# Row maxima of the attention stage from the high parts alone: two chunks side by side in the two row halves of TensorE's array

## The reference, cut to what matters

```python
q = jnp.einsum('qdh,bcd->bhcq', Q, x) * sq
k = jnp.einsum('qdh,bcd->bhcq', K, x) * sq
v = jnp.einsum('vdh,bcd->bhcv', V, x) * sv
att = jnp.einsum('bhcq,bhCq->bhcC', q, k) / d_query
att = jnp.where(causal, att, -jnp.inf)
p = jax.nn.softmax(att, axis=-1)
y = jnp.einsum('bhcC,bhCv->bhcv', p, v)
z = jnp.einsum('dvh,bhcv->bcd', W, y) * (math.sqrt(d_embed / d_value) / num_heads)
```

## Time and profile before

| | |
|---|---|
| median of 3 runs | 2350.81 us (2349.38 to 2351.51) |
| profiled execution: own time, span | 2350.51 us, 2348.7 us |
| TensorE matmul busy, weight loads | 2008.2 us (86%), 1419.8 us (60%) |
| VectorE, ScalarE, GpSimd busy | 1377.0 us, 1007.6 us, 1166.8 us |
| attention stage | about 740 to 2050 us of the span |

### The profile page before, as it was taken

The page is one execution under the profiler, slowest core; times in us unless marked ns, Lnnn a source line. Parts: engine busy times, 40 slices in busy tenths (PEclk is TensorE's granted clock), DMA queues, the critical chain, the costliest instruction groups (busy, mean ns, idle before and its releaser), DMA issues. The chain is left out here.

```text
span 2348.7 us, 42315 instructions
## 1 busy us (share of the span) xinstructions
PE 2008.2 (86%) x11537; PEld 1419.8 (60%) x11538; DVE 1377.0 (59%) x3643; ACT 1007.6 (43%) x2116; POOL 1166.8 (50%) x1160
## 2 busy tenths in 40 slices
PE   4653999998957999989999989999999999956650
PEld 2352666665635777767777767777667777645550
DVE  7753333332345666665777665778656778647761
ACT  2210333332323555555555544555545555513540
POOL 0055222222211665643668753667744677826882
PEclk8855999999977999999999989999999999967985
DMA  8194222234240111111122101112102121123978
GB/s 306 65 291 173 43 47 45 45 82 109 45 136 18 47 47 50 46 30 44 47 69 52 47 27 45 49 51 53 47 22 53 44 56 45 38 90 122 198 115 239
DMA packets 234313, 186.45 MB, mean 79 GB/s; under 512 B 102826, under 2 KB 222471, under 8 KB 232592
## 3 DMA queue, kind: packets, MB, share of 16 engines
q1 hardware_dynamic: 200816, 149.15, 21.9%
q0 software_dynamic: 29088, 30.89, 8.2%
q10 hardware_dynamic: 4224, 4.19, 0.5%
HBM read 101.74 MB, written 82.95 MB: 79 GB/s over the span
## 5 line engine op out<-in xcount | busy, mean ns | idle before, releaser
L884 POOL TENSOR_TENSOR c_den<-c_den,c_p 128x512 f32<-128x512 f32 (+3 forms) x576 | 551.1, 957 | 358.8 <-ACT c_p L1113 288.0
L1113 ACT ACTIVATE c_p<-PS 128x512 f32<-128x512 f32 (+3 forms) x768 | 350.2, 487 | 349.4 <-PE PS L2183 237.1
L2204 PE MATMUL PS<-c_p,c_vh 128*64 128x256 f32 (+1 forms) x2816 | 336.1, 352 | 0.0
L2152 PE MATMUL PS<-c_k,c_q 128*128 128x512 f32 (+2 forms) x768 | 290.8, 380 | 29.9 <-DVE c_max L1606 20.4
L2175 PE MATMUL PS<-c_q,c_k 128*128 128x512 f32 (+2 forms) x768 | 292.9, 385 | 3.1 <-issue 1.9
L827 POOL DMA_INDIRECT acc<-b_y,b_tok x72 | 111.1, 1543 | 331.7 <-ACT b_y L1024 303.5
L2054 PE MATMUL PS<-b_w12T,b_tT 128*128 x576 | 272.9, 597 | 1.5 <-ACT b_tT L1007 0.7
L2204 PEld LDWEIGHTS PS<-c_p,c_vh 128*64 128x64 f32 x2816 | 198.4, 137 | 107.0 <-issue 53.5
L2176 PE MATMUL PS<-c_q,c_k 128*128 128x512 f32 (+2 forms) x768 | 259.0, 348 | 0.0
L1104 ACT ACTIVATE c_q<-PS 64x512 fp32r<-64x512 f32 x256 | 150.9, 590 | 176.2 <-PE PS L2139 173.0
L1613 DVE CUSTOM_DVE_ANT_0 PS<-PS,c_maskq 128x128 f32<-128x128 f32 (+3 forms) x256 | 127.0, 501 | 145.3 <-PE PS L2152 139.1
(11 more groups left out here) (286 smaller groups left out, 3611.2 us busy)
## 6 DMA issues: line engine op xcount, KB each, us to landing
c_vh<-c_v SPq DMA_DIRECT2D x64, 256.0 KB
c_rrow<-rden SPq DMA_DIRECT2D x64, 256.0 KB, 3.5
b_xt<-routed SPq DMA_DIRECT2D x72, 130.0 KB, 2.1
routed<-b_empty SPq DMA_DIRECT2D x32, 289.0 KB, 7.6
d_xe<-routed SPq DMA_DIRECT2D x32, 289.0 KB, 3.9
b_w12T<-in_w12T_dram SPq DMA_DIRECT2D x16, 512.0 KB, 12.7
acc<-X SPq DMA_DIRECT2D x16, 512.0 KB, 2.9
X<-acc SPq DMA_DIRECT2D x16, 512.0 KB, 9.5
```

The costliest lines, as they stand in the source:

```text
L884: pool.tensor_tensor(c_den[c][:, off:], c_den[c][:, off:], p, ALU.add).then_inc(s_cPa, 1)
L1113: act.activation(c_p[:, P_AT[m]:P_AT[m] + WIDTH[m]], PS[:, ST_BANK[m % ROUND], skip:skip + WIDTH[m]], ACT.Exp, scale=ATT_SCALE).then_inc(s ...
L2152: pe.matmul(PS[:, 2 + use[0], 0:max(w, 256)], c_q1[h][:, t * P:(t + 1) * P], c_k1[h][:, c * 512:c * 512 + max(w, 256)], start=True, stop=T ...
L2204: ins = pe.matmul(dst, c_vh[h][:, j, :], moving, start=(j == 0), stop=(t0 == 2 + a))
```

## The change

The chunks of the first pass multiply high parts alone: each matmul is 64 rows deep. Even chunks use rows 0 to 63 of `c_q1` and `c_k1`, odd chunks rows 64 to 127 of `c_q1` and `c_k2`, so that two neighbouring chunks stand in different row halves of the array. In the built program such a matmul has the tile size 64 x 128, at row 0 or row 64. For this `c_k2` has the high keys in rows 64 to 127, written by a fourth ScalarE copy from bank 0, and the ones in row 0; `c_q2` has the low queries in rows 64 to 127 and the maxima in row 0. GpSimd's copy goes. The chunks are issued in pairs, and the order on TensorE changes for it.

```diff
@@ SyncE
-                sp.dma_start(c_q2[h][DQ:DQ + 1, :].rearrange("a (t q) -> a t q", t=QT).bitcast(F32),
+                sp.dma_start(c_q2[h][0:1, :].rearrange("a (t q) -> a t q", t=QT).bitcast(F32),
@@ GpSimd
-            def copy_k(H, h):
-                pool.wait_ge(s_cqs, H * 6 + 6)
-                pool.sem_inc(s_pass, 1)
-                pool.tensor_copy(c_k2[h][0:DQ, :], c_k1[h][0:DQ, :].bitcast(F32)).then_inc(s_ck2, 1)
-                    if m == 4 and (nxt or hd + 1 < NH):
-                        copy_k(H + 1, 1 - h)
@@ ScalarE
-                            (c_k1[h][0:DQ, cols], PS[DQ:P, 0, :]))[part]
+                            (c_k1[h][0:DQ, cols], PS[DQ:P, 0, :]), (c_k2[h][DQ:P, cols], PS[DQ:P, 0, :]))[part]
-                    splits_hi(0, 2)
+                    splits_hi(0, 2, 3)
-                splits_hi(1, 0, 1, 2)
+                splits_hi(1, 0, 1, 2, 3)
@@ VectorE
-                dst, rows, hi = ((c_q2[h][0:DQ, cols], slice(0, DQ), c_q1[h]), (c_k1[h][DQ:P, cols], slice(DQ, P), c_k1[h]))[k]
-                dve.wait_ge(s_cqs, H * 6 + (c * 3 + k + 2))
-                dve.tensor_tensor(dst, PS[rows, 0, :], hi[0:DQ, cols].bitcast(F32), ALU.subtract).then_inc(s_cks, 1)
+                dst, rows, hi = ((c_q2[h][DQ:P, cols], slice(0, DQ), c_q1[h]), (c_k1[h][DQ:P, cols], slice(DQ, P), c_k2[h]))[k]
+                dve.wait_ge(s_cqs, H * 8 + (c * 4 + 2 * k + 2))
+                dve.tensor_tensor(dst, PS[rows, 0, :], hi[rows, cols].bitcast(F32), ALU.subtract).then_inc(s_cks, 1)
@@ TensorE
-                pe.matmul(PS[:, 2 + use[0], 0:max(w, 256)], c_q1[h][:, t * P:(t + 1) * P], c_k1[h][:, c * 512:c * 512 + max(w, 256)],
-                          start=True, stop=True).then_inc(s_cS, 1)
+                half = slice(n % 2 * DQ, (n % 2 + 1) * DQ)
+                pe.matmul(PS[:, 2 + use[0], 0:max(w, 256)], c_q1[h][half, t * P:(t + 1) * P],
+                          (c_k1, c_k2)[n % 2][h][half, c * 512:c * 512 + max(w, 256)], start=True, stop=True).then_inc(s_cS, 1)
-                    pe.wait_ge(s_ck2, H + 1)
...
-                maxima(4)
+                maxima(4, 5)
                 scores_t(H, h, 4)
-                maxima(5)
...
-                maxima_ahead(0)
+                denominators(H, 0)
+                maxima_ahead(0, 1)
                 projections(5)
-                maxima_ahead(1)
-                denominators(H, 0)
                 outputs_of(2)
```

More of the change, by code:

```diff
@@ L391, in network @@
         s_cks = sem("c_qk_lo_ready")
-        s_ck2 = sem("c_k2_ready")
         s_cv = sem("c_v_ready")
@@ L513, in batch_order @@
                 fetch = nxt and hd == NH - 2
-                order = ["M4", "M5", "M6"] * follows + ["X0", "X1"] * fetch + ["M7"] * follows
+                order = ["M4", "M5", "M6", "M7"] * follows + ["X0", "X1"] * fetch
                 order += ["Z2", "Z3"] * (zs and hd % 2 == 1)
@@ L904, in _ @@
                 pool.tensor_copy(dst, r_swb[:, cols]).then_inc(s_dcast, 1)
-            pool.wait_ge(s_cset, 3)
-            copy_k(0, 0)
             batch_adds(0, False, True)
@@ L1055, in _ @@
             for m in c_q2 + c_k2:
-                st.done(act.activation(m[DQ:P, :], zeros[DQ:P, 0:1].broadcast_to([P - DQ, S]), ACT.Copy))
+                st.done(act.activation(m[0:P - DQ, :], zeros[0:P - DQ, 0:1].broadcast_to([P - DQ, S]), ACT.Copy))
             st.sync()
@@ L1159, in head_exps @@
                     take_xT(b + 1, 1, table)
-                    splits_hi(0, 0, 1, 2)
+                    splits_hi(0, 0, 1, 2, 3)
                 take_y(H, pair, h, 0, c_yT[hp % 2])
@@ L1192, in _ @@
             for H, c in ((0, 0), (0, 1), (1, 0)):
-                for part in range(3):
+                for part in range(4):
                     split_hi(H, H, c, part)
             take_max(0, first_turns())
-            for part in range(3):
+            for part in range(4):
                 split_hi(1, 1, 1, part)
@@ L1767, in head_steps @@
                     invert(H - 1, 1 - h)
-                maxima(6)
+                maxima(6, 7)
                 if fetch:
                     low_xT(b + 1, 0, table)
-                maxima(7)
                 if h == 1 and zs:
@@ L1825, in _ @@
             for h in range(2):
-                st.done(dve.memset(c_k2[h][DQ:DQ + 1, :].bitcast(F32), 1.0))
+                st.done(dve.memset(c_k2[h][0:1, :].bitcast(F32), 1.0))
             st.sync()
@@ L2297, in head_products @@
                 scores_t(H, h, 5)
-                maxima(6)
                 if fetch:
+                    maxima(6, 7)
                     transpose_x(b + 1, 0, table)
-                    maxima(7, 8)
                 else:
-                    projections(0)
-                    maxima(7)
-                    projections(1)
+                    projections(0, 1)
+                    maxima(6, 7)
                     if h == 1:
@@ L2308, in head_products @@
                     projections(2)
-                    maxima(8)
                 outputs_of(0)
+                maxima(8, 9)
                 scores_t(H, h, 6)
-                maxima(9)
                 scores_t(H, h, 7)
-                maxima(10)
                 scores_t(H, h, 8)
                 mask_t(8)
-                maxima(11)
+                maxima(10, 11)
                 if fetch:
@@ L2334, in head_products @@
                 projections(3, 4)
-                maxima_ahead(0)
+                denominators(H, 0)
+                maxima_ahead(0, 1)
                 projections(5)
-                maxima_ahead(1)
-                denominators(H, 0)
                 outputs_of(2)
-                maxima_ahead(2)
                 if follows:
                     scores_t(H + 1, 1 - h, 0)
-                maxima_ahead(3)
+                maxima_ahead(2, 3)
                 if follows:
```

## The result

The changed kernel takes 2495.43 us (2495.36 to 2496.17, 4 runs) against 2350.1 us in the same runs: a ratio of 1.0611, 95% interval 1.0588 to 1.0633, 145 us slower. The direction was forecast, the size was not: 66 us were expected, and 2495 lies above the range.

What follows compares the result with a forecast made beforehand. TensorE's matmul steps were taken to bound the attention stage. Switches less overlap (+23.3 and +31.0 us) and the fourth copy's delay (+11.3) gave +65.6 on 2350.5: 2416 us, 2.8% slower, range 2305 to 2455 for 8 in 10.

Steps and rivals of the forecast that it cites:

- TensorE's steps bound the stage.: Attention stage: time is the sum of TensorE's steps, so changes to them reach the end nearly one for one.
- 17.2 us: Profile before: read as TensorE's longest wait for a maximum, in five places.
- TensorE would stay busy at 97%: Expected profile after: TensorE busy at 97% in an attention stage about 65 us longer.
- Pairs overlap whole.: First-pass pairs: both matmuls run at once, the shorter costs nothing, saving 0.95 us a head.
- A switch costs 0.20, rows as well as columns.: TensorE, into or out of a pair: 0.09 us stall plus 0.11 us exposed load at every switch.
- The net of both, +54 us: TensorE's added switches less overlap: +23.3 us for the M pairs and +31.0 us for the N pairs.
- The fourth copy delays T by 0.18 us a head, 11 us.: ScalarE's added copy delays VectorE's low keys, then M11's maximum and TensorE's transposes of the maxima: +11.3 us.
- A pair also needs both banks emptied ... so I take no further wait, with up to 0.2 us a head (13 us) above.: Between pairs, six other matmuls or a products block against about two VectorE reductions: no added wait, at most 13 us.
- free: Rival: row changes on TensorE are no switch; the pairs save 59.6 us, 2291 to 2317 us; chance 0.18.
- with the load hidden: Rival: a switch costs only the 0.09 us stall, loads pulled ahead; 2359 us, between 2347 and 2367; chance 0.14.
- Halves that don't overlap: Rival: a pair's two matmuls run one after the other, 0.95 us a head unsaved; 2476 us; chance 0.08.

Runs made afterwards that it cites:

- e4: Kernel before, in its own order, each first-pass chunk only 64 rows deep, all in rows 0 to 63: 2621.9 us, +228 us against the kernel before.
- e11: Kernel before, no pairs, each first-pass chunk's matmul and maximum cut to its first 256 columns: 2340.35 us, -53 us against the kernel before.
- e8: Kernel before, with only GpSimd's second key copy done by ScalarE as a fourth copy: 2361.23 us, +9 us against the kernel before.
- e5: Changed kernel, fourth copy read from c_k1, VectorE's low keys waiting for three copies: 2486.07 us, +134 us against the kernel before.
- e6: Changed kernel, M6/M7 one projection step earlier and Z one later in odd heads: 2474.6 us, +123 us against the kernel before.
- e2: Changed kernel, each maximum taken over the first 64 columns of its chunk only: 2457.03 us, +63 us against the kernel before.
- e10: Changed kernel with e5 and e6 joined, M4/M5 ahead of the denominators, N0/N1 ahead of the products with the values: 2458.81 us, +65 us against before.
- e9: Changed kernel, M10/M11 behind the products with the values, except in the head that fetches: 2534.13 us, +182 us against the kernel before.
- e7: Changed kernel's layout and copies, only M8/M9 and M10/M11 as pairs, other chunks 128 rows deep: 2426.16 us, +33 us against the kernel before.

## Why the prediction was wrong, point by point

- *TensorE's steps bound the stage.* Right for the kernel before: e4 took 1 us more than its switches were priced at, and e11 gave back what its columns were, inside its range. One row was misread on the way: 17.2 us is the sum of five waits, the longest of them is 5.8. That TensorE would stay busy at 97% didn't come true: 1366 of 1450 us are 94%.
- *Pairs overlap whole.* Right: two in 0.50 us, the second 3 to 4 ns behind the first. *A switch costs 0.20, rows as well as columns.* Right: +228 for +227 in e4. The net of both, +54 us, measured +48 to +57.
- *The fourth copy delays T by 0.18 us a head, 11 us.* Right where it stands alone (e8, +9). In the changed kernel T loses 20 us, and e5 shows that it isn't the copy, so this term came out for another reason than the one given.
- *"A pair also needs both banks emptied ... so I take no further wait, with up to 0.2 us a head (13 us) above."* This step failed: about 90 us of added waits, where the sum had none for the banks and 11 at T. I counted TensorE's matmuls between two pairs against two reductions of VectorE. That left out four things. Z uses the same two banks and stands right behind M6/M7 in the new order (26 us; e6 takes it away). VectorE's program has routing steps between the maxima of M8 and M9, whose bank M11 needs (26 us; e2 takes most of it away). M4/M5 wait for VectorE's low keys and for its addition of Z1 (27 us more than before; e10 shows that a later place takes most of it away, and what is waited for is read from the trace). T waits for a chain through VectorE that begins with M8 (20 us; e2 and e9). One by one before, TensorE hardly waited for a chunk's bank (5 places, 17.2 us); two at once ask also for the bank that was filled last.

The two rivals with cheaper switches, free or with the load hidden, fall with e4. Halves that don't overlap, 2476 us, came nearest to the time, and for a reason that isn't the case.

## What to carry to other kernels

Where two buffers alternate, issuing their users two at a time takes the slack of one whole use away from the engine that empties them; count that engine's program from buffer to buffer, with everything that stands between the two and everyone else who uses the buffers, not the number of instructions on the fast side. And a division of the array pays only where a run of divided matmuls is long against the two switches around it: here 0.40 us of switches stand against 0.12 to 0.23 us saved, so a pair between two whole-array matmuls loses even with no wait at all, and a pair beside a column block, which adds one switch, about breaks even (e7).

## What the runs showed of the hardware that was not expected

Two 64-row matmuls that write the same PSUM partitions in two banks run side by side at full speed, and so do their weight loads (two loads in 0.19 us, as one alone takes). A switch between whole rows and half rows costs what one between whole columns and half columns does, 0.09 of stall and 0.11 of load, in either direction (e4: 0.33 into a single chunk, 0.43 out of it and 0.33 to the next, where each is 0.23 without a switch).
